# The opening of a cross-attention kernel in another order

## The reference

```python
text_ehs, ip_ehs = ehs[:, :-4], ehs[:, -4:]
q, k_t, v_t = heads(x @ W_q), heads(text_ehs @ W_k), heads(text_ehs @ W_v)
probs_t  = softmax(einsum('bhsd,bhtd->bhst', q, k_t) * 8 ** -0.5)
text_out = einsum('bhst,bhtd->bhsd', probs_t, v_t)
k_ip, v_ip = heads(ip_ehs @ W_k_ip), heads(ip_ehs @ W_v_ip)
attn_scores = einsum('bhsd,bhnd->bhsn', q, k_ip) * 8 ** -0.5
qsem = l2norm(einsum('bhst,bte->bhse', probs_t, text_ehs))
sem  = einsum('bhse,bne->bhsn', qsem, l2norm(ip_ehs))
probs_ip = softmax(attn_scores + 0.5 * sem) * spatial_mask[None, None, :, None]
ip_out = einsum('bhsn,bhnd->bhsd', probs_ip, v_ip)
out = (text_out + ip_out) @ W_out + b_out + x
```

## Time and profile before

| | |
|---|---|
| median of 3 runs | 226.52 us (226.52 to 226.81) |
| profiled execution | 225.47 us |
| its span, first to last instruction | 223.5 us |
| mean granted PE clock | 0.992 |
| busy, share of the span | PE 94%, DVE 82%, ACT 77%, POOL 67% |
| the chain that ended last | PE 68%, DVE 9%, DMA 8% |

### The profile page before, as it was taken

The page is one execution under the profiler, slowest core; times in us unless marked ns, Lnnn a source line. Parts: engine busy times, 40 slices in busy tenths (PEclk is TensorE's granted clock), DMA queues, the critical chain, the costliest instruction groups (busy, mean ns, idle before and its releaser), DMA issues.

```text
span 223.5 us, 6984 instructions
## 1 busy us (share of the span) xinstructions
PE 210.6 (94%) x1619; PEld 197.6 (88%) x1619; DVE 183.7 (82%) x1147; ACT 172.7 (77%) x569; POOL 149.3 (67%) x255
## 2 busy tenths in 40 slices
PE   8986859999999999999999999999999999998984
PEld 8876749999899999989999999999999999997973
DVE  4726529797988979697979899897979797999893
ACT  2608739897987979788888889697988888897831
POOL 2152301929688696959696977969696969698870
PEclk9996999999999999999999999999999999999999
DMA  5530553555462644565454647264545455461101
GB/s 137 110 121 18 115 148 72 146 142 155 128 164 70 193 112 124 147 158 149 135 155 121 181 103 198 76 181 109 153 123 158 148 144 149 105 167 32 47 1 44
DMA packets 47340, 27.60 MB, mean 123 GB/s; under 512 B 8513, under 2 KB 45538, under 8 KB 47322
## 3 DMA queue, kind: packets, MB, share of 16 engines
q1 hardware_dynamic: 46682, 26.96, 44.8%
q10 hardware_dynamic: 640, 0.43, 0.8%
HBM read 10.14 MB, written 1.52 MB: 52 GB/s over the span
## 4 chain that ended last, share of the span: by engine, by line
PE 68%; DVE 9%; DMA 8%; POOL 4%; issue 4%; ACT 3%; SPq 3%; DVEq 0%; POOLq 0%; ACTq 0%
PE main_ps L952 13%; PE main_ps L954 12%; PE probsT_ps L934 11%; DMA main_rhs<-g_stage 8%; PE pa L924 8%; PE score_ps L984 6%; PE pb L1012 4%; DVE junk L713 3%; PE pb L1024 3%; PE pa L1031 2%; PE main_ps L870 2%; PE pa L1039 2%; POOL rnorm L500 2%; SPq L373 1%; PE probsT_ps L865 1%
## 5 line engine op out<-in xcount | busy, mean ns | idle before, releaser
L612 ACT ACTIVATE probs<-score_ps,negmax 128x124 f32<-128x124 f32 x320 | 93.2, 411 | 1.1 <-DVE negmax L778 1.0
L713 DVE CUSTOM_DVE_ANT_0 junk<-main_ps,probs 128x124 f32<-128x124 f32 x320 | 77.8, 280 | 2.5 <-PE main_ps L954 2.0
L952 PE MATMUL main_ps<-main_rhs,probsT 124*128 124x137 f32 x320 | 64.8, 283 | 2.7 <-DVE small L715 2.7
L954 PE MATMUL main_ps<-main_rhs,probsT 124*128 124x137 f32 x320 | 63.3, 279 | 0.0
L500 POOL TENSOR_TENSOR rnorm<-clamped,exponent 128x20 f32<-128x20 f32 x15 | 53.2, 3544 | 1.2 <-DVE clamped L698 1.2
L778 DVE TENSOR_REDUCE negmax<-score_ps 128x4 f32<-128x496 f32 x80 | 53.1, 663 | 0.0
L952 PEld LDWEIGHTS main_ps<-main_rhs,probsT 124*128 124x128 f32 x320 | 48.9, 190 | 4.5 <-ACT probsT L565 2.0
L565 ACT ACTIVATE probsT<-probsT_ps 124x512 f32<-124x512 f32 x80 | 50.9, 636 | 2.5 <-PE probsT_ps L934 1.7
L934 PE MATMUL probsT_ps<-ident_sb,probs 128*124 128x128 f32 x320 | 49.0, 276 | 0.0
L954 PEld LDWEIGHTS main_ps<-main_rhs,probsT 124*128 124x128 f32 x320 | 48.7, 188 | 0.0
L934 PEld LDWEIGHTS probsT_ps<-ident_sb,probs 128*124 128x124 f32 x320 | 39.1, 141 | 5.3 <-issue 0.4
(11 more groups left out here) (165 smaller groups left out, 343.5 us busy)
## 6 DMA issues: line engine op xcount, KB each, us to landing
main_rhs<-g_stage SPq DMA_DIRECT2D x16, 660.0 KB, 4.2
vrep<-vip_d SPq DMA_DIRECT2D x13, 320.0 KB, 3.6
k_diag<-k_stack SPq DMA_DIRECT2D x60, 64.0 KB, 2.2
ctxT_sb<-ctxT SPq DMA_DIRECT2D x16, 124.0 KB, 2.7
xT_sb<-xT SPq DMA_DIRECT2D x16, 80.0 KB, 2.1
xn_sb<-xn SPq DMA_DIRECT2D x15, 80.0 KB, 2.0
out<-out_sb SPq DMA_DIRECT2D x15, 80.0 KB, 1.7
k_diag<-k_stack SPq DMA_DIRECT2D x60, 16.0 KB, 1.8
```

The costliest lines, as they stand in the source:

```text
L612: last = act.activation(probs[p][:, h, :], score_ps[(p * G + g) % 2][:, j * TOK:j * TOK + T], ACT.Exp, bias=negmax[p][:, h:h + 1])
L713: dve.tensor_tensor_reduce(junk[:, 2 * r + a, :], u, probs[wb][:, h, :], 1.0, 0.0, ALU.mult, ALU.add, norm2[wb][:, h:h + 1])
L952: pe.matmul(main_ps[r][:, 0:MAIN], probsT[mp][:, 2 * r, :], blk[:, RW - MAIN:RW], start=True, stop=True)
L954: pe.matmul(main_ps[r][:, MAIN:2 * MAIN], probsT[mp][:, 2 * r + 1, :], blk[:, 0:MAIN], start=True, stop=True).then_inc(s_main, 1)
```

## The change

All of it lies in the prologue and window 0; from window 1 on each engine does the same in the same order.

- Loads: W_q ahead of the image key weights on ACT's queue; on SP's the queries of batch 0 ahead of `zip_sb`, and the image tokens and their value weights behind batch 1's loads.
- PE: 5 warm-up products in place of 10. q of batch 0 ahead of the image keys, its transposes ahead of those of k. G of batch 0 is made at once, without image columns, with v in one bank. Batch 0's first two scores come ahead of batch 1's projections; the image projections (`project_ip`) behind these, with the image columns of batch 0's G as a product of its own, 4 columns wide. Batch 1's k transposes go to g = 3 and its q transposes to g = 4.
- ACT: G and v of batch 0 before its q and k copies. Of batch 1, `g_stage`, `v_stage` and the high part of k (now `gkv_stages`) go behind the second group's exponentials, `k_stack` to g = 4, `q_stack` (`q_stacked`) to the window's end.
- DVE: in window 0 `kip_split` and its neighbours behind the third group's maximum, then k's and q's remainders. New is `sp_first`, the copy of the four image columns.
- POOL: clears `k_diag[1]` in its first fills; instead of the image columns in `ctxT_sb[0]` it spreads `sp_first` into `main_rhs[0]`.
- SP: batch 0's `main_rhs` copy takes 124 columns instead of 132.

```diff
         @block.sync
         def _(sp):
             sp.dma_start(ctxT_sb[0][:, :, 0:T], ctxT[0]).then_inc(s_ctx_in[0], 16)
+            sp.dma_start(xT_sb[0][:, :, :], xT[0]).then_inc(s_xT_in[0], 16)
             sp.wait_ge(s_zip, 1)
             sp.dma_start(zip_sb[0][:, :, T:TOK], ipT[:, :, 0:NIP]).then_inc(s_zip_in[0], 16)
-            sp.dma_start(xT_sb[0][:, :, :], xT[0]).then_inc(s_xT_in[0], 16)
...
             sp.dma_start(wkv_sb[:, :, 0:C], wkv[:, :, 0:C]).then_inc(s_wv_in, 16)
-            sp.dma_start(ipT_sb[:, :, :], ipT).then_inc(s_ipT_in, 16)
-            sp.dma_start(wkvip_sb[:, :, C:2 * C], wkvip[:, :, C:2 * C]).then_inc(s_wvip_in, 16)
             sp.dma_start(ctxT_sb[1][:, :, 0:T], ctxT[1]).then_inc(s_ctx_in[1], 16)
             sp.wait_ge(s_zip, 3)
             sp.dma_start(zip_sb[1][:, :, T:TOK], ipT[:, :, NIP:2 * NIP]).then_inc(s_zip_in[1], 16)
             sp.dma_start(xT_sb[1][:, :, :], xT[1]).then_inc(s_xT_in[1], 16)
+            sp.dma_start(ipT_sb[:, :, :], ipT).then_inc(s_ipT_in, 16)
+            sp.dma_start(wkvip_sb[:, :, C:2 * C], wkvip[:, :, C:2 * C]).then_inc(s_wvip_in, 16)
             sp.wait_ge(s_gstage, 1)
-            sp.dma_start(main_rhs[0][:, :, D + 1:D + 1 + NIP + TOK],
-                         g_stage[:, :].unsqueeze(1).broadcast_to([TOK, NPAIR, NIP + TOK])).then_inc(s_grep[0], 16)
+            sp.dma_start(main_rhs[0][:, :, D + 1 + NIP:D + 1 + TOK],
+                         g_stage[:, NIP:TOK].unsqueeze(1).broadcast_to([TOK, NPAIR, T])).then_inc(s_grep[0], 16)
...
+                    if w == 0:
+                        sp.wait_ge(s_vipT_mm, 1)
                     wait(sp, s_ctx_mm, b + 1)
                     sp.dma_start(ctxT_sb[p][:, :, 0:T], ctxT[b + 2]).then_inc(s_ctx_in[p], 16)
...
                 pool.memset(bass.AP(main_rhs[n], D, [[NPAIR * RW, TOK], [RW, NPAIR], [RW - 2 * D - 1, 2]]), 1.0)
+            pool.memset(k_diag[1][:, :, :, :].bitcast(F32), 0.0).then_inc(s_zeros[1], 1)
             pool.memset(oT[:, :, :], 1.0).then_inc(s_fill, 1)
...
-            pool.wait_ge(s_ipunitT, 1)
-            pool.wait_ge(s_k0_mm, 1)
-            pool.tensor_copy(ctxT_sb[0][:, :, T:TOK], ipunitT[:, :, 0:NIP]).then_inc(s_ipcol, 1)
             pool.wait_ge(s_v0, 1)
             v_columns(0)
-            pool.memset(k_diag[1][:, :, :, :].bitcast(F32), 0.0).then_inc(s_zeros[1], 1)
+            pool.wait_ge(s_ipunitT, 1)
             pool.wait_ge(s_k1_mm, 1)
             pool.tensor_copy(ctxT_sb[1][:, :, T:TOK], ipunitT[:, :, NIP:2 * NIP]).then_inc(s_ipcol, 1)
+            pool.wait_ge(s_sp_first, 1)
+            pool.tensor_copy(bass.AP(main_rhs[0], D + 1, [[NPAIR * RW, TOK], [RW, NPAIR], [TOK, 2], [1, NIP]]),
+                             sp_first[:, :].unsqueeze(1).unsqueeze(1).broadcast_to([TOK, NPAIR, 2, NIP])).then_inc(s_spcol, 1)
...
         def _(act):
             act.dma_start(wkv_sb[:, :, C:2 * C], wkv[:, :, C:2 * C]).then_inc(s_wk_in, 16)
+            act.dma_start(wq_sb[:, :, :], wq).then_inc(s_wq_in, 16)
             act.dma_start(wkvip_sb[:, :, 0:C], wkvip[:, :, 0:C]).then_inc(s_wkip_in, 16)
-            act.dma_start(wq_sb[:, :, :], wq).then_inc(s_wq_in, 16)
             act.wait_ge(s_wq_in, 16)
             act.activation(wq_scaled[:, :, :], wq_sb[:, :, :], ACT.Copy, scale=SCALE).then_inc(s_wq, 1)
+            act.wait_ge(s_q_mm, 1)
+            act.activation(q_split[:, :, 0, :, :], doubled(probsT_ps[1][:, 0:C]), ACT.Copy).then_inc(s_qhi, 1)
             act.wait_ge(s_k0_mm, 1)
             act.activation(k_split[:, :, :, 0, :], doubled(probsT_ps[0][:, 0:C]), ACT.Copy).then_inc(s_khi, 1)
-            act.wait_ge(s_q_mm, 1)
-            act.activation(q_split[:, :, 0, :, :], doubled(probsT_ps[1][:, 0:C]), ACT.Copy).then_inc(s_qhi, 1)
+            act.wait_ge(s_ctx_mm, 1)
+            act.activation(g_stage[:, NIP:TOK], score_ps[1][:, 0:T], ACT.Copy).then_inc(s_gstage, 1)
+            act.activation(v_stage[:, :], score_ps[1][0:T, TOK:TOK + C], ACT.Copy).then_inc(s_v0, 1)
+            act.wait_ge(s_qT, 1)
+            act.activation(q_stack[0][:, 0:G - 1, :].rearrange("r g t -> r (g t)"), main_ps[1][:, :],
+                           ACT.Copy).then_inc(s_qst03, 1)
             act.wait_ge(s_kT, 1)
             act.wait_ge(s_zeros[0], 1)
...
             for j in range(2):
                 rows = slice(32 * j, 32 * j + 32)
                 act.activation(k_diag[0][rows, G - 1, j, :], pb[rows, 0:TOK], ACT.Copy).then_inc(s_kd4[0], 16)
-            act.wait_ge(s_qT, 1)
-            act.activation(q_stack[0][:, 0:G - 1, :].rearrange("r g t -> r (g t)"), main_ps[1][:, :],
-                           ACT.Copy).then_inc(s_qst03, 1)
-            act.wait_ge(s_qlo, 1)
-            act.activation(v_stage[:, :], probsT_ps[1][0:T, C:2 * C], ACT.Copy).then_inc(s_v0, 1)
-            act.wait_ge(s_ctx_mm, 1)
-            act.activation(g_stage[:, NIP:NIP + TOK], pa[:, 0:TOK], ACT.Copy)
-            act.activation(g_stage[:, 0:NIP], pa[:, T:TOK], ACT.Copy).then_inc(s_gstage, 1)
...
+                    if g == 0 and has(w, ahead=1) and w != 0:
+                        gkv_stages(b, p, i, w)
+                    if g == 3 and has(w, ahead=1) and w != 0:
+                        q_stacked(b, n)
...
-                    if g == 1 and has(w, ahead=1):
+                    if g == (4 if w == 0 else 1) and has(w, ahead=1):
...
-                    if g == 0 and has(w, ahead=1):
+                    if g == 1 and w == 0:
+                        gkv_stages(b, p, i, w)
+                    if g == (1 if w == 0 else 0) and has(w, ahead=1):
                         wait(act, s_q_mm, b + 2)
                         act.activation(q_split[:, :, 0, :, :], doubled(pb[:, 0:C]),
                                        ACT.Copy).then_inc(s_qhi, 1)
+                    if g == 4 and w == 0:
+                        q_stacked(b, n)
...
-                    if g == 2 and has(w, ahead=1):
+                    if g == (3 if w == 0 else 2) and has(w, ahead=1):
...
                     if g == 2 and w == 0:
                         dve.wait_ge(s_vipT_mm, 1)
+                        dve.tensor_copy(sp_first[:, :], main_ps[0][:, BANK - NIP:BANK]).then_inc(s_sp_first, 1)
                         kips = doubled(main_ps[0][0:B * NIP, 0:C])
                         dve.tensor_copy(kip_split[:, :, :, 0, :].bitcast(F32R), kips).then_inc(s_kip, 1)
...
-                    if g == 0 and has(w, ahead=1):
+                    if g == (2 if w == 0 else 0) and has(w, ahead=1):
...
             pe.wait_ge(s_warm, 1)
-            for k in range(10):
+            for k in range(5):
                 pe.matmul(main_ps[1][:, 0:128], warm[:, :], warm[:, :], start=True, stop=True)
             pe.wait_ge(s_ctx_in[0], 16)
             pe.wait_ge(s_zip, 2)
             pe.wait_ge(s_wk_in, 16)
             project(probsT_ps[0][:, 0:C], ctxT_sb[0], lambda c: wkv_sb[:, c, C:2 * C], True, False)
+            pe.wait_ge(s_xT_in[0], 16)
+            pe.wait_ge(s_wq, 1)
+            project(probsT_ps[1][:, 0:C], xT_sb[0], lambda c: wq_scaled[:, c, :], True, True).then_inc(s_q_mm, 1)
             pe.wait_ge(s_zip_in[0], 16)
             pe.wait_ge(s_wkip_in, 16)
             project(probsT_ps[0][:, 0:C], zip_sb[0], lambda c: wkvip_sb[:, c, 0:C], False, True).then_inc(s_k0_mm, 1)
-            pe.wait_ge(s_xT_in[0], 16)
-            pe.wait_ge(s_wq, 1)
-            project(probsT_ps[1][:, 0:C], xT_sb[0], lambda c: wq_scaled[:, c, :], True, True)
+            project(score_ps[1][:, 0:TOK], ctxT_sb[0], lambda c: ctxT_sb[0][:, c, :], True, True)
             pe.wait_ge(s_wv_in, 16)
-            project(probsT_ps[1][:, C:2 * C], ctxT_sb[0], lambda c: wkv_sb[:, c, 0:C], True, True).then_inc(s_q_mm, 1)
+            project(score_ps[1][:, TOK:TOK + C], ctxT_sb[0], lambda c: wkv_sb[:, c, 0:C], True, True).then_inc(s_ctx_mm, 1)
...
-            mm.then_inc(s_vipT_mm, 1)
-            pe.wait_ge(s_ipcol, 1)
-            pe.wait_ge(s_kst03, 1)
-            pe.wait_ge(s_kd03[0], 64)
-            project(pa[:, 0:TOK], ctxT_sb[0], lambda c: ctxT_sb[0][:, c, :], True, True).then_inc(s_ctx_mm, 1)
+            def project_ip():
...
+                pe.wait_ge(s_qst03, 1)
+                for x in range(2):
+                    project(main_ps[0][0:B * NIP, x * C:(x + 1) * C], ipT_sb, lambda c: wkvip_sb[:, c, x * C:(x + 1) * C],
+                            True, True)
...
+                pe.wait_ge(s_ipunitT, 1)
+                project(main_ps[0][:, BANK - NIP:BANK], ctxT_sb[0], lambda c: ipunitT[:, c, 0:NIP], True,
+                        True).then_inc(s_vipT_mm, 1)
...
                     if w == 0:
                         pe.wait_ge(s_vipT, 1)
+                        pe.wait_ge(s_spcol, 1)
...
-                    if g == 0 and w == 0:
+                    if g == 1 and w == 0:
                         pe.wait_ge(s_ctx_in[1], 16)
-                        pe.wait_ge(s_gstage, 1)
+                        pe.wait_ge(s_kd03[0], 64)
...
```

(35 more changed lines are left out.)

75 lines of the change are left out of this document (44 added, 31 removed).

## The result

The changed kernel takes 228.59 us (median of 8 runs, 228.11 to 229.97), the kernel before 226.54 (8 runs, 226.46 to 227.66). The ratio is 1.0089, interval 1.0057 to 1.0121: slower by some 2 us, where the forecast was 225.4, 1.1 us faster. The profiled execution took 228.41 us, its span is 226.4; before, 225.47 and 223.5. Ratios here leave out executions over 1.5% above the fastest of their kernel, among them far outliers (1201.35 us in e3, 350.22 in e4, 348.07 in e7); medians count all.

What follows compares the result with a forecast made beforehand. The opening's chain through SP's queue (kip_d, k_diag, main_rhs) was taken to bound the kernel; the gate 1.07 earlier made 225.47 less 1.1, 224.4, or 225.4 by the median; bounds 224.8 to 225.9, 8-in-10 range 224.6 to 226.8.

Steps and rivals of the forecast that it cites:

- The bound: Opening: SP's queue from kip_d through batch 1's k_diag and main_rhs copies holds ACT; a shift reaches the end whole.
- the gate: When ACT may write g_stage again because batch 1's main_rhs has landed; forecast 30.73 instead of 31.80.
- Parts 3 and 4: Third score to kip_d (19.57, 1.19 earlier), then kip_d to batch 1's k_diag (23.76, 1.07 earlier) and g_stage (30.73).
- Part 1: PE's opening up to the first score: forecast at 11.0, 1.2 us earlier than before.
- Five warm-up products fewer ... cost or save nothing of themselves.: PE's start, before q: the shortened warm-up was priced at nothing, its effect on the clock left to a rival.
- q cannot start before 5.6: PE's q of batch 0 waits for scaled W_q, ready at 5.6; the reason given for the shorter warm-up costing nothing.
- Rival 1: PE stays at 1.2 GHz until behind v: 1.6 us more, 227.0; a halfway rise costs 0.8, 226.2; chance 17%.
- Part 2: PE from first to third score, with batch 1's and the moved image projections between: third score at 17.14.
- The four small rows: PE's new 4-column rows, image columns of batch 0's G, ahead of the third score: 0.37 to 0.54, taken as 0.45.
- Rival 2: PE's clock falls in its idle time, about 18.4 to 19.8, costing up to 2.4 before k_stack; 227.2; chance 7%.
- Rival 3: The gain is lost behind the gate because q_stack, ACT's last copy in window 0, is late; 226.5; chance 8%.
- The sum: Whole kernel: profiled execution 225.47 less 1.1 gives 224.4; in terms of the median, 1.05 above, 225.4.

Runs made afterwards that it cites:

- e3: e1 plus four zero products on PE where it waits for the first score; 226.10 us, 0.9962 of the kernel before.
- e4: Kernel before with DVE's block on the image keys (kip_split, vip_sb, vipT_sb) moved directly behind the first group's maximum; 223.13 us, 0.9835 of before.
- e7: Changed kernel with 10 warm-up products, project_ip ahead of first score, early kip_split, window 0 mostly in old order, batch 1's G/v/k copies earlier; 220.57 us, 0.9732 of before.
- e1: Changed kernel with 10 warm-up products in place of 5, nothing else; 226.39 us, 0.9988 of the kernel before.
- e6: The changed kernel run once more, unaltered; 228.81 us against 226.66 for the kernel before.
- e2: Kernel before with 5 warm-up products instead of 10, nothing else; 229.59 us, 1.0114 of the kernel before.
- e5: e4 with six zero products in PE's idle time ahead of batch 1's key transposes; 221.07 us, 0.9752 of the kernel before.
- e11: e7's kernel with 15 warm-up products in place of 10; 220.90 us, 0.9728 of the kernel before.

## Why the prediction was wrong

- **The bound** was read rightly. SP's queue, kip_d, the k_diag copies and the landing of main_rhs set the gate, and a shift there reaches the end: in the changed kernel 2.7 us of delay passed through Parts 3 and 4 to within 0.2, and e4, which sends kip_d 5.66 us earlier, is 3.5 us faster.
- **Part 1, the failed step: "Five warm-up products fewer ... cost or save nothing of themselves."** Against the forecast it measured 1.13 us to the first score, since image k, G and most of v ran at the 1.2 GHz level; against the same program with 10 it is 1.59 (12.13 and 10.54, e1), and 2.2 to 2.4 by the medians (228.59 and 228.81 against 226.39). That is over two thirds of the 3.2 us between forecast and measurement. The reason given, that q cannot start before 5.6, did not hold either: W_q was scaled by 5.28, and q's start at 5.55 is the end of text k's slow rows. In the same way image k's 6.62 is the end of q's slow rows, and zip_sb had landed by 5.9 (issued at 2.36, at most 3.5 to landing). That both starts agree with the forecast to 0.1 is luck.
- **Rival 1** named this mechanism at 17%, and at 227.0. It was true, whole, and too cheap: the price was counted once, up to v. What no rival priced is the wait for `k_diag` ahead of the first score, which the change itself makes: before, the image projections and G filled that time (9.80 to 12.22). Behind the empty 1.24 to 1.25 us the level fell in all three traces that have it (the changed kernel, e1, e6); with zero products there (e3), or with the image projections (the kernel before, e2, e4, e5, e7 to e11), it did not.
- **Part 2** took 7.85 us from the first score to the third, not 6.14; the difference is batch 1's three projections and the two scores at half rate. In e3, without that fall, it took 6.18. The four small rows took 0.45, as estimated.
- **Rival 2** looked for a second fall at 18.4 to 19.8. The wait it spoke of came, 1.19 us from 21.58, and PEclk read 1.00 behind it up to 33.70. Falls came elsewhere: behind the wait ahead of the first score, and again behind the gate, where the same length of idle time had not cost the level in the profile of before. That the level would hold behind the gate was an unsaid term; it cost some 1.3 more.
- **Rival 3**, a gain lost behind the gate, is what e3 shows in part: the gate is 0.74 earlier than before, the time 0.4% lower and hardly outside its interval. The cause was not q_stack but the low stretch.
- **The sum.** 225.47 - 1.1 was to be 224.4; the execution took 228.41. The 4.0 between are 2.7 at the gate and 1.3 behind it. By the medians it is 3.2 (228.59 against 225.4): the profiled execution of before was 1.05 faster than its kernel's median, that of the changed kernel only 0.18, so 0.8 of the 4.0 is the draw of executions. The range's upper end, 226.8, held Rival 1's half, not its whole and nothing on top.

The Trainium skill, "TensorE: Matmul & The Clock Gate", Part 1, puts the price of the slow start below 1% of a typical kernel's span. Here five products fewer cost 1.14% (e2, 0.71 to 1.57); in the trace of e2 the slow rows stand ahead of the first score and further low stretches follow. The Trainium skill says in the same section that the number of slow products at the start varies from run to run. The traces agree: with 10 warm-up products the rise came between 4.8 and 7 us.

Open: why one idle time costs the level and another does not; its length alone does not tell (1.24 cost it in e1, 1.83 did not in the kernel before). e3 against e1 separates the fall before the first score, but their times do not differ beyond their intervals; in e5 the fall came although most of the idle time was filled. The stretch behind the gate was seen but never taken away by itself, so its 1.3 us is read from one pair of traces.

## What to carry to other kernels

Warm-up products are not decoration to be cut when the loads they cover come sooner: what counts is the level at which the rows behind them run, so price a shorter warm-up by the rows up to the first proof of the upper level, and add each later wait of PE that the new order leaves. A row that is moved away from a wait takes its cover with it. Where a chain of waits sets the opening, look first for the engine that idles while its result is the chain's head: moving one block on DVE (e4) was worth more than reordering four engines. And test the parts of a reordering singly: taking the warm-up alone (e1, e2) showed its price, while the worth of G at once is still unknown, because e7 changed it together with other things.
